# Between the two attentions of a decoder: batch 0's chain alone in front, batch 1's under its scatters and under the first expert items

## The chip, the cores and the metric

One Trainium2 chip, of which one core runs the program. The metric is the device time of one execution in microseconds (us); lower is better. Spans, waits and clocks are from the hardware profiler's record of one execution.

## The reference, cut to what matters

A decoder of two layers on x of 2 x 1024 x 256 (batch, sequence, width), all in float32. What lies between the two self-attentions of the program is the rest of layer 0, and this is the part that is changed:

```python
x = x + _L0_attn_ref(_layernorm(x, axis=-1), ...)             # its last product: s @ w_o
x = x + _L0_xattn_ref(ctx_1024, _layernorm(x, axis=-1), ...)  # a window of 4 out of 77 context rows
x = x + _L0_ffn_ref(_layernorm(x, axis=-1), ...)              # 8 experts, top 2, capacity 320

# cross attention: where a token looks, then scores against 77 context rows
hid = jnp.tanh(jnp.einsum('btc,pc->btp', c_t, W_p))
p_t = Sq * jax.nn.sigmoid(jnp.einsum('btp,op->bto', hid, V_p))
...
gauss = jnp.exp(-jnp.square(s_pos - p_t) / (2.0 * STAN_DEV ** 2))
a_t = jax.nn.softmax(scores, axis=-1) * gauss
s_t = jnp.einsum('btw,btwq->btq', a_t, qw)
# mixture of experts: routing, then a batch's rows of each expert (at most 320), then two matrices up and one down
_, selected_experts = jax.lax.top_k(expert_weights, K)
count_fused = jnp.cumsum(mask_fused, axis=1)
trunc_mask = expert_mask * (count <= capacity).astype(jnp.int32)
h1 = jnp.einsum('ebcm,emh->ebch', dispatch, w1)
h3 = jnp.einsum('ebcm,emh->ebch', dispatch, w3)
expert_out = jnp.einsum('ebch,ehm->ebcm', jax.nn.silu(h1) * h3, w2)
```

The routing of a batch (its running count) needs all 1024 tokens of that batch and none of the other.

## The kernel before

The program runs in stages with a barrier between them: layer 0's attention, then the stage that is called `middle`, then layer 1's attention, then a tail. `middle` handles 16 tiles of 128 tokens, tiles 0 to 7 of batch 0 and 8 to 15 of batch 1, in groups of four tiles (groups 0 and 1 are batch 0's, 2 and 3 batch 1's). Its steps stand in one list, and each engine walks the same list and does its share of each step, so the list sets the order on every engine:

- `turn` and `out`: the attention's heads transposed, times w_o, added to x (TensorE L1534, L1545; VectorE L1808).
- `stat`, `shift`, `norm`: layer norm. VectorE takes mean and variance (L1817 to L1828), ScalarE the root (L1666) and writes the normed rows `xn_nat` (L1674), TensorE transposes them (L1553), ScalarE copies the first half out of PSUM (L1679) and VectorE the second (L1833). Units 0 to 3 are the groups' first norm, units 4 to 7 (`norm 4` and so on) the second, ahead of the experts.
- `hid`, `pos`, `mask`, `score`, `sum`, `flip`, `value`: cross attention (TensorE L1561, L1569, L1576, L1583, L1590). `mask` is thirteen small VectorE instructions in a row (L1841 to L1854), `score` three (L1859 to L1861), `sum` four (L1867 to L1871).
- `logit`, `best`, `cum`, `slot`: routing of a batch (TensorE L1601, L1607 to L1610; VectorE L1788 to L1922). `slot` ends with `idx_s`, the row in DRAM to which each token goes.
- Then GpSimd scatters the batch's normed rows to DRAM (`disp`, L1734) with 16 indirect DMAs.
- An item is one expert with the rows of one batch (320 rows) or of both (640). `rows` loads them from `disp` by SP's queue (L1469) and transposes them (L1619, `xeT`), `ffn` is 7 steps of the two upward products (L1632, four matmuls a batch; a float32 matmul shows as two instructions) with ScalarE's Silu (L1725) and VectorE's product (L1928, `hT`), `y` the downward product (L1642) and its copy (L1944, L1947), which GpSimd stores (L1749).

Weights of two experts are held. SP loads the next expert's upward matrices when TensorE has ended the last `ffn` step of an expert's last item, and the downward one after that item's `y` (L1452, L1455). After the last items GpSimd gathers the results (L1756) and VectorE adds them to x (L1782).

ScalarE holds one table of functions at a time. Tanh and Exp share one, the root and Silu need others, and a copy needs none; a change shows as ACT_TABLE_LOAD.

The list of before has three parts. `lead` is batch 0's chain with `turn 2`, `out 2` and `turn 3` of batch 1 between its steps. `rest` is batch 1's chain from `out 3` to its last `value`; it runs while batch 0 is scattered, and stands ahead of the first `rows` step. `under` is batch 1's second norm and its routing, and is dealt out between the steps of the first item, one TensorE step after each. The items are 12:

```python
    items = [(0, (0,)), (1, (0,)), (0, (1,)), (1, (1,))] + [(e, (0, 1)) for e in range(2, E - 2)] + [
        (E - 2, (0,)), (E - 1, (0,)), (E - 2, (1,)), (E - 1, (1,))]
```

## Time and profile before

| what | us |
|---|---|
| median of 3 runs (lowest, highest) | 1929.97 (1928.99, 1933.12) |
| the profiled execution | 1936.54 |
| its span | 1934.8 |
| granted TensorE clock, mean over the span | 0.906 of full |
| TensorE busy in the span | 1622.1 (84%) |
| VectorE, ScalarE, GpSimd busy | 1049.7, 875.7, 554.9 |

The profiled execution is 1.7 us longer than its span, which runs from its first to its last instruction. The stage `middle` takes from 411.7 us of the span to its barrier at about 1013.7. In the rows below a time at the start of a line is in us from the start of the span. PE is TensorE's matmuls and PEld its weight loads, DVE VectorE, ACT ScalarE, POOL GpSimd, SPq SP's queue. PEclk 1.00 is a granted clock of 2.4 GHz and 0.50 one of 1.2 GHz.

### The profile page before, as it was taken

To read this page: it belongs to the slowest core of one execution; us is meant where nothing else is said; L and a number is where in the kernel's file an instruction comes from. 1 tells how busy PE (TensorE), PEld (TensorE's weight loads), DVE (VectorE), ACT (ScalarE), POOL (GpSimd) and SP (SyncE) were. 2 spreads that over 40 slices of the span, in tenths; PEclk is the share of its full clock that TensorE was granted. 3 is DMA by queue.
4 is the path that set the end of the run, shared out by engine and by line. 5 is a ranking of instruction groups with operands and counts; after the bars stand their busy time and mean duration, and the time that the engine had idled before them with its cause. 6 is when DMAs were issued, how large, how long until landed. Compare 5 with 4: busy or idle time off the path is not lost. (4 is left out here: it accounts for less than half of the span.)

```text
span 1934.8 us, 34483 instructions
## 1 busy us (share of the span) xinstructions
PE 1622.1 (84%) x12814; PEld 1092.5 (56%) x12814; DVE 1049.7 (54%) x2134; ACT 875.7 (45%) x1467; POOL 554.9 (29%) x791
## 2 busy tenths in 40 slices
PE   4668899876576999999927819999999999997888
PEld 2323333335454777777713406777777777776644
DVE  4557777624441111111236328888888888884556
ACT  2115666653231111111106108888888887883431
POOL 2201111110303000000333115556555565553011
PEclk9759999987677999999967659999999999998899
DMA  2541121030101232221213286687786886854100
GB/s 82 124 156 22 22 43 22 2 120 1 51 7 64 84 116 85 84 78 54 64 52 129 82 109 194 181 201 200 204 208 193 205 210 193 201 172 157 72 12 33
DMA packets 207560, 207.44 MB, mean 107 GB/s; under 512 B 20612, under 2 KB 186131, under 8 KB 207267
## 3 DMA queue, kind: packets, MB, share of 16 engines
q1 hardware_dynamic: 202531, 191.61, 37.1%
q0 software_dynamic: 4864, 13.64, 2.1%
q8 instruction: 103, 1.69, 0.4%
q14 instruction: 62, 0.51, 0.1%
HBM read 123.18 MB, written 81.81 MB: 106 GB/s over the span
## 5 line engine op out<-in xcount | busy, mean ns | idle before, releaser
L1174 DVE CUSTOM_DVE_ANT_0 prob<-ps,dev 128x1024 f32<-128x1024 f32 x256 | 311.5, 1218 | 30.3 <-DMA dev<-skew_u 27.4
L1072 ACT ACTIVATE prob<-prob,nmax 128x1024 f32<-128x1024 f32 x256 | 293.5, 1146 | 38.4 <-DVE nmax L1174 38.2
L1004 PE MATMUL ps<-cst,prob 128*128 128x128 f32 x2048 | 279.1, 277 | 1.1 <-ACT probT L1079 0.9
L1004 PEld LDWEIGHTS ps<-cst,prob 128*128 128x128 f32 x2048 | 227.3, 141 | 44.0 <-issue 21.6
L1632 PE MATMUL ps<-xeT,w 128*128 128x320 f32 x896 | 246.8, 436 | 5.0 <-ACT xeT L1713 5.0
L723 ACT ACTIVATE pT<-ps 128x512 f32<-128x512 f32 (+3 forms) x384 | 166.1, 495 | 153.3 <-PE ps L683 150.9
L1188 DVE COPY probT<-ps 128x512 f32<-128x512 f32 x256 | 176.3, 689 | 102.9 <-PE ps L1004 102.9
L760 DVE TENSOR_REDUCE nmax<-ps 128x1 f32<-128x128 f32 (+7 forms) x256 | 185.2, 754 | 82.1 <-PE ps L664 80.9
L1632 PEld LDWEIGHTS ps<-xeT,w 128*128 128x128 f32 x896 | 170.1, 191 | 76.9 <-ACT xeT L1713 5.2
L1079 ACT ACTIVATE probT<-ps 128x512 f32<-128x512 f32 x256 | 151.3, 591 | 102.1 <-PE ps L1004 102.1
L1725 ACT ACTIVATE sg<-ps 128x320 f32<-128x320 f32 (+1 forms) x84 | 44.2, 526 | 330.4 <-PE ps L1632 328.7
L987 PE MATMUL ps<-ks,qs 96*128 96x512 bf16 (+4 forms) x768 | 155.7, 312 | 33.5 <-DVE nmax L1174 22.3
L1928 DVE TENSOR_TENSOR hT<-ps,sg 128x320 f32<-128x320 f32 (+1 forms) x84 | 50.6, 603 | 197.6 <-ACT sg L1725 190.9
L1642 PE MATMUL ps<-w,hT 128*128 128x256 f32 (+1 forms) x616 | 140.7, 388 | 5.9 <-DVE hT L1928 5.8
L662 PE MATMUL ps<-ks,qs 96*128 96x512 bf16 (+3 forms) x384 | 111.5, 356 | 38.1 <-DVE nmax L760 25.4
L1045 PE MATMUL ps<-probT,vg 128*18 128x128 f32 (+1 forms) x4096 | 135.9, 273 | 0.0
L1642 PEld LDWEIGHTS ps<-w,hT 128*128 128x128 f32 (+1 forms) x616 | 112.1, 185 | 31.6 <-DVE hT L1928 7.8
L747 POOL TENSOR_SCALAR_AFFINE_SELECT pT<-pT 128x512 f32<-128x512 f32 x64 | 40.8, 637 | 282.9 <-ACT pT L723 282.9
L683 PE MATMUL ps<-qs,ks 99*128 99x512 bf16 (+3 forms) x384 | 110.2, 337 | 13.6 <-ACT pT L723 7.3
L1045 PEld LDWEIGHTS ps<-probT,vg 128*18 128x18 f32 (+1 forms) x4096 | 106.4, 98 | 17.3 <-issue 16.9
L1749 POOL DMA_DIRECT2D ybuf<-ye x32 | 20.5, 644 | 319.6 <-DVE ye L1944 180.8
L1128 POOL TENSOR_TENSOR wm<-wr,cst 128x256 f32<-128x256 f32 x128 | 94.0, 734 | 43.9 <-DMA wr<-skew_p 41.0
(310 smaller groups left out, 2247.9 us busy)
## 6 DMA issues: line engine op xcount, KB each, us to landing
dev<-skew_u SPq DMA_DIRECT2D x128, 256.0 KB, 3.5
skew_p<-prob SPq DMA_DIRECT2D x128, 256.0 KB, 3.3
w<-in_L_ffn_w SPq DMA_DIRECT2D x24, 896.0 KB, 6.3
skew_u<-cst SPq DMA_DIRECT2D x64, 256.0 KB, 4.1
wr<-skew_p SPq DMA_DIRECT2D x128, 128.0 KB, 3.0
qs<-qd SPq DMA_DIRECT2D x96, 128.0 KB, 3.9
ks<-kd SPq DMA_DIRECT2D x48, 256.0 KB, 6.0
qd<-parts SPq DMA_DIRECT2D x48, 128.0 KB, 1.8
```

The costliest lines, as they stand in the source:

```text
L662: last = nc.tensor.matmul(ps[:, bank, 0:hi - lo], query, ks[0:KS, j, lo:hi], start=True, stop=hi < w)
L723: nc.scalar.activation(pT[:, c % 2, r, 0:w], ps[:, ring_bank(job), 0:w], ACT.Exp).then_inc(s_exp, 1)
L760: nc.vector.tensor_reduce(nmax[:, n % 2, r * KB + a:r * KB + a + 1], slot[:, 0:w], AX.X, ALU.max, negate=True).then_inc(s_max, 1)
L987: last = nc.tensor.matmul(ps[:, 2 * (t % 2) + lo // 512, lo % 512:lo % 512 + hi - lo], qs[:, n % 2, r, a * P:(a + 1) * P], ks[:, n % 2, r, ...
L1004: last = nc.tensor.transpose(ps[:, ring_bank(job), kb * P:(kb + 1) * P], prob_tile(t, (4 * h + kb) * P, (4 * h + kb + 1) * P), k.c("ident"))
L1045: last = nc.tensor.matmul(ps[r * VW:r * VW + wide, 7, q % 4 * P:q % 4 * P + P], vg[:, n % 2, r, kb, int(kb == a), 0:wide], probT[:, (HQ * ...
L1072: nc.scalar.activation(prob_tile(t, 0, S), prob_tile(t, 0, S), ACT.Exp, bias=nmax[:, t % 4:t % 4 + 1], scale=-1.0).then_inc(s_exp, 1)
L1079: nc.scalar.activation(probT[:, t % SLOTS, 0:512], ps[:, ring_bank(job), :], ACT.Copy).then_inc(s_evA, 1)
L1174: nc.vector.tensor_tensor_reduce(out=prob_tile(t, 0, S), in0=scores, in1=dev_tile(t), scale=-1.0, scalar=3.0e38, op0=ALU.add, op1=ALU.min, ...
L1188: nc.vector.tensor_copy(probT[:, t % SLOTS, 512:S], ps[:, ring_bank(job), :]).then_inc(s_evD, 1)
L1632: last = nc.tensor.matmul(ps[:, banks(job)[0] + z * wide + h, 0:CAP], w[:, e % 2, c, f * P:(f + 1) * P], xeT[:, c, h * CAP:(h + 1) * CAP], ...
L1642: last = nc.tensor.matmul(ps[0:w, banks(job)[0] + t // 2, t % 2 * D:(t % 2 + 1) * D], hT[:, f, o:o + w], w2[:, e % 2, f, :], start=(f == 0 ...
```

## The change

`middle` becomes `experts`. Batch 0 and batch 1 get a chain each (class `RowChain`), with buffers and semaphores of their own, and the same steps in the same order (`chain_order`). Batch 0's chain stands in front with nothing of batch 1 in it. Five lots of spare transposes (`warm`: 10, 16, 20, 6 and 20 of the identity, into a bank that nobody reads) stand ahead of five of its steps on TensorE. Then comes batch 1's chain up to `hid 3`, then the first `rows`. All that follows of batch 1's chain is dealt out between the steps of the items, up to two TensorE steps after each. The normed rows are written by GpSimd in place of ScalarE, for both batches, and ScalarE copies both halves of a norm's transposes out of PSUM in place of one. The items are 13: experts 0, 1, 2 for batch 0, then 2, 1, 0 for batch 1, then 3, 4, 5 for both, then 6 and 7 for each. Since the weights of two experts are held, those of expert 0 are loaded a second time, for the sixth item. `sg` and `yg` lie in buffers of batch 0's chain.

```diff
-def middle_order(items):
+def chain_order(b):
...
+    g, h = 2 * b, 2 * b + 1
+    return (two("turn", g) + [("prep", b)] + two("out", g) + two("turn", h) + [("stat", g)] + two("out", h) + [("shift", g), ("stat", h)] +
...
+        kind = step[0]
+        if kind == "shift":
+            u = step[1]
+            at = self.slots(u).start
+            pool.wait_ge(self.s_shift, self.normed.index(u) + 1)
...
+                nc.gpsimd.tensor_scalar(self.xn[:, t, :], k.x[:, KB * self.b + t, :], self.rstd[:, at + j:at + j + 1],
+                                        self.shift[:, at + j:at + j + 1], ALU.mult, ALU.add).then_inc(self.s_xs, 1)
...
+def warmed(steps, where):
+
+    return [s for step in steps for s in ([("warm", where[step], step)] if step in where else []) + [step]]
+
+
+def experts_order(items, lead, chain, ahead):
+
+
+    begun = chain.index(("hid", 3)) + 1
+    under = list(chain[begun:])
+    order = list(lead) + list(chain[:begun]) + [("rows", 0)]
+
+    def deal():
+        singles = 0
+        while under and singles < 2:
+            order.append(under.pop(0))
+            singles += order[-1][0] in RowChain.SINGLE
+
...
+    AHEAD = 3
+    items = ([(e, (0,)) for e in range(AHEAD)] + [(e, (1,)) for e in reversed(range(AHEAD))] +
+             [(e, (0, 1)) for e in range(AHEAD, E - 2)] + [(E - 2, (0,)), (E - 1, (0,)), (E - 2, (1,)), (E - 1, (1,))])
...
+        order = experts_order(items, warmed(chains[0].order, {("norm", 0, 0): 10, ("flip", 0): 16, ("norm", 4, 0): 20, ("norm", 5, 0): 6, ("cum", 0): 20}), chains[1].order, AHEAD)
...
+                for n in range(len(items)):
+                    if n in (0, AHEAD):
+                        sp.wait_ge(chains[n // AHEAD].s_sc, 16 * 2 * KB)
...
+                    if n and last_use[use[n - 1]] == n - 1 and use[n - 1] + 2 < len(loads):
+                        i = use[n - 1] + 2
+                        sp.wait_ge(s_job, done(("ffn", n - 1, FC0 - 1)))
+                        load_up(i)
+                        sp.wait_ge(s_job, done(("y", n - 1)))
+                        load_down(i)
...
+                    if kind == "warm":
+                        for _ in range(step[1]):
+                            nc.tensor.transpose(ps[:, 7, 0:P], k.c("ident"), k.c("ident"))
```

The first place is TensorE in batch 0's chain, from its two `score` steps to its first `logit`. `turned` and `wo` are the `out` step's operands, `x_sc` the scores, `xn_nat` and `xn_c` the normed rows. The row of `cst` alone is a lot of spare transposes. Before:

```order
L1576 MATMUL ps<-gT,xT 128x77 x8
L1561 MATMUL ps<-xT,wpT 100x512 x2
L1569 MATMUL ps<-vp,hidT 128x1 x4
L1534 MATMUL ps<-cst,xT 128x128 x8
L1576 MATMUL ps<-gT,xT 128x77 x8
L1583 MATMUL ps<-cst,x_sc 77x128 x4
L1545 MATMUL ps<-wo,turned 128x256 x8
L1583 MATMUL ps<-cst,x_sc 77x128 x4
L1590 MATMUL ps<-ctxn,aT 128x256 x8
```

and after:

```order
L1473 MATMUL ps<-gT,xT_c 128x77 x8
L1468 MATMUL ps<-vp,hidT_c 128x1 x4
L1473 MATMUL ps<-gT,xT_c 128x77 x8
L1876 MATMUL ps<-cst 128x128 x16
L1477 MATMUL ps<-cst,x_sc_c 77x128 x8
L1481 MATMUL ps<-ctxn,aT_c 128x256 x8
L1876 MATMUL ps<-cst 128x128 x20
L1460 MATMUL ps<-cst,xn_c 128x128 x8
L1486 MATMUL ps<-gateT_c,xT_c 128x8 x8
```

Batch 1's `turn` (L1534) and its `out` of eight matmuls (L1545) are gone from between the steps, the two `flip` steps stand together, and two lots of spare transposes have come in.

The second place is TensorE at the first item. L1632 before and L1902 after are the upward products, `x4` being one of the seven steps of an item with one batch; what stands between them is batch 1's chain. Before, where it is the second norm and `logit`:

```order
L1632 MATMUL ps<-xeT,w 128x320 x4
L1553 MATMUL ps<-cst,xn_nat 128x128 x4
L1632 MATMUL ps<-xeT,w 128x320 x4
L1553 MATMUL ps<-cst,xn_nat 128x128 x4
L1632 MATMUL ps<-xeT,w 128x320 x4
L1601 MATMUL ps<-gateT,xT 128x8 x8
L1632 MATMUL ps<-xeT,w 128x320 x4
```

and after:

```order
L1902 MATMUL ps<-xeT,w 128x320 x4
L1473 MATMUL ps<-gT,xT_c 128x77 x8
L1468 MATMUL ps<-vp,hidT_c 128x1 x4
L1902 MATMUL ps<-xeT,w 128x320 x4
L1473 MATMUL ps<-gT,xT_c 128x77 x8
L1477 MATMUL ps<-cst,x_sc_c 77x128 x4
L1902 MATMUL ps<-xeT,w 128x320 x4
L1477 MATMUL ps<-cst,x_sc_c 77x128 x4
L1481 MATMUL ps<-ctxn,aT_c 128x256 x2
L1902 MATMUL ps<-xeT,w 128x320 x4
L1481 MATMUL ps<-ctxn,aT_c 128x256 x4
```

Scores, `flip` and `value` of batch 1, which stood ahead of the first item, now stand inside it, two steps in each gap.

The third place is GpSimd from batch 0's scatter to batch 1's. `xn_c` are the normed rows, four to a unit, and `ybuf` an item's stored result. Before:

```order
L1734 DMA disp<-xn_nat,idx_s 2688x256 x16
L1741 TENSOR_TENSOR x_gs<-cst,x_pt 128x308
L1744 TENSOR_TENSOR x_gs<-x_gs 128x308
L1741 TENSOR_TENSOR x_gs<-cst,x_pt 128x308
L1744 TENSOR_TENSOR x_gs<-x_gs 128x308
L1734 DMA disp<-xn_nat,idx_s 2688x256 x16
```

and after:

```order
L1562 DMA disp<-xn_c,idx_s_c 2688x256 x16
L1549 TENSOR_SCALAR xn_c<-x,rstd_c,shift_c 128x256 x8
L1554 TENSOR_TENSOR x_gs_c<-cst,x_pt_c 128x308
L1557 TENSOR_TENSOR x_gs_c<-x_gs_c 128x308
L1554 TENSOR_TENSOR x_gs_c<-cst,x_pt_c 128x308
L1557 TENSOR_TENSOR x_gs_c<-x_gs_c 128x308
L1549 TENSOR_SCALAR xn_c<-x,rstd_c,shift_c 128x256 x8
L1949 DMA ybuf<-ye 128x2x256
L1949 DMA ybuf<-ye 64x256
L1562 DMA disp<-xn_c,idx_s_c 2688x256 x16
```

Batch 1's normed rows are now written by GpSimd, and its first eight wait in GpSimd's queue behind the 16 scatters of batch 0.

## Rows read from the trace of the kernel before

**Rows 1.** Windows of the stage: length; PE, PEld, DVE, ACT, POOL busy us (instructions); PEclk, DMA, GB/s.

```profile
411.70:498.30 86.60, 58.36 (x250) 47.17 (x251) 38.53 (x138) 26.41 (x48) 2.85 (x4) 0.70 0.19 67
498.30:550.50 52.20, 28.14 (x112) 20.60 (x110) 27.59 (x94) 15.66 (x32) 18.53 (x20) 0.66 0.16 53
550.50:636.20 85.70, 65.98 (x273) 48.92 (x273) 15.58 (x53) 15.05 (x29) 16.82 (x18) 0.84 0.11 36
636.20:980.40 344.20, 338.25 (x1387) 251.86 (x1386) 63.39 (x103) 47.38 (x92) 33.30 (x44) 1.00 0.24 79
```

**Rows 2.** Timeline, two items of one batch in a row.

```profile
902.73 15.34 PE L1632 MATMUL ps<-xeT,w 128*128 128x320 f32 x56
...
928.60 15.34 PE L1632 MATMUL ps<-xeT,w 128*128 128x320 f32 x56
```

**Rows 3.** Timeline of batch 0's chain: start, duration, engine, line, what.

```profile
439.20 0.16 DVE L1841 TENSOR_SCALAR x_pt<-x_pt 128x4 f32<-128x4 f32 x1
...
443.23 0.48 DVE L1859 TENSOR_TENSOR x_sc<-ps,x_tmp 128x308 f32<-128x308 f32 x1
...
455.18 5.21 PE L1545 MATMUL ps<-wo,turned 128*128 128x256 f32 x16
...
463.08 3.62 PE L1590 MATMUL ps<-ctxn,aT 77*128 77x256 f32 x16
...
473.03 2.10 PE L1553 MATMUL ps<-cst,xn_nat 128*128 128x128 f32 x8 [5.46 <-ACT xn_nat L1674]
...
476.12 3.55 PE L1601 MATMUL ps<-gateT,xT 128*128 128x8 f32 x16 [0.99 <-DVE xT L1833]
...
484.29 3.55 PE L1601 MATMUL ps<-gateT,xT 128*128 128x8 f32 x16 [0.83 <-issue]
...
498.09 0.17 DVE L1922 CAST idx_s<-r_sl 128x16 uint32<-128x16 f32 x1
```

**Rows 4.** Timeline from batch 1's first norm to the first item.

```profile
505.74 2.08 ACT L1674 ACTIVATE xn_nat<-x,shift,rstd 128x256 f32<-128x256 f32 x4
...
515.03 1.93 PE L1561 MATMUL ps<-xT,wpT 128*100 128x512 f32 x4
...
544.12 1.46 PE L1619 MATMUL ps<-cst,xe 128*128 128x128 f32 x6
...
550.58 4.08 PE L1632 MATMUL ps<-xeT,w 128*128 128x320 f32 x8 [5.00 <-ACT xeT L1713]
```

**Rows 5.** Timeline of TensorE's two longer waits in the first items.

```profile
577.29 0.43 PE L1607 MATMUL ps<-r_cand,cst 128*128 128x64 f32 x2 [4.38 <-DVE r_cand L1893]
...
623.15 1.52 PE L1619 MATMUL ps<-cst,xe 128*128 128x128 f32 x6 [15.26 <-DMA xe<-disp]
```

**Rows 6.** Groups by form on GpSimd: busy us, mean ns of one, idle before.

```profile
L215 POOL TENSOR_SCALAR x<-x,inv0a,shift0a 128x256 f32<-128x256 f32 x16 | 8.8, 560 | 28.3 <-ACT xs0a L202 28.3
```

**Rows 7.** Window of the chain's second half.

```profile
473.00:499.00 26.00, 18.73 (x74) 16.45 (x75) 8.34 (x38) 7.90 (x13) 0.43 (x1) 0.50 0.00 1
```

**Rows 8.** Groups by line from 440 to 625 us: busy us, mean ns.

```profile
L1734 POOL DMA_INDIRECT disp<-xn_nat,idx_s x32 | 31.1, 973 | 128.1 <-DVE idx_s L1922 119.0 <-issue 9.1
...
L1601 PE MATMUL ps<-gateT,xT 128*128 128x8 f32 x64 | 10.8, 306 | 1.8 <-DVE xT L1833 1.0 <-issue 0.8
...
L1590 PE MATMUL ps<-ctxn,aT 77*128 77x256 f32 x32 | 10.7, 505 | 0.0
...
L1553 PE MATMUL ps<-cst,xn_nat 128*128 128x128 f32 x48 | 9.7, 353 | 13.2 <-ACT xn_nat L1674 7.1 <-issue 6.0
...
L1576 PE MATMUL ps<-gT,xT 128*128 128x77 f32 x57 | 9.3, 329 | 0.0
...
L1725 ACT ACT_TABLE_LOAD x2 | 2.6, 1283 | 0.0
```

**Rows 9.** Timeline and window of an expert's upward weights being loaded.

```profile
651.56 0.90 SPq L1452 DMA_DIRECT2D w<-in_L_ffn_w  x2
...
654.00:658.00 4.00, 4.00 (x20) 3.51 (x20) 0.00 (x0) 0.00 (x0) 0.00 (x0) 1.00 0.96 393
```

More of the change, by code:

```diff
@@ new lines, in chain_order @@
+    g, h = 2 * b, 2 * b + 1
+    return (two("turn", g) + [("prep", b)] + two("out", g) + two("turn", h) + [("stat", g)] + two("out", h) + [("shift", g), ("stat", h)] +
+            two("norm", g) + [("shift", h), ("hid", g)] + two("norm", h) + [("pos", g), ("hid", h), ("mask", g), ("score", g), ("pos", h),
+            ("mask", h), ("score", h), ("sum", g), ("flip", g), ("sum", h), ("flip", h)] + two("value", g) + [("stat", 4 + g)] +
+            two("value", h) + [("shift", 4 + g), ("stat", 4 + h)] + two("norm", 4 + g) + [("shift", 4 + h), ("logit", g)] +
+            two("norm", 4 + h) + [("logit", h), ("best", b), ("cum", b), ("slot", b)])
@@ L1318, in middle_order @@
             order.append(("ffn", n, f))
[L1319 to L1322 removed]
+            deal()
         if n + 1 < len(items):
@@ L1401, in middle @@
+        own = [s for s in jobs if s[0] not in RowChain.SINGLE]
+        singles = [s for s in jobs if s[0] in RowChain.SINGLE]
+        lead = where[("rows", 0)]
+        split = max(n for n in range(len(items)) if ("ffn", n, 0) in jobs[:where[("cum", 1)]]) + 1
+        assert split <= AHEAD
         xe = k.sb("xe", [P, ST, D], ctx=ctx)
         xeT = k.sb("xeT", [P, DC, ROWS], ctx=ctx)
-        sg = k.sb("sg", [P, 2, ROWS], ctx=ctx)
+        sg = chains[0].xT[:, 0:2, 0:ROWS]
         hT = k.sb("hT", [P, FC0, ROWS], ctx=ctx)
@@ L1422, in pieces, with tenants, place, done @@
+        def tenants(i):
+            return sorted({max(had) for q in bank[i] if (had := [j for j in range(i) if q in bank[j]])})
+        def place(step):
+            return [s for s in own if s[0] == step[0]].index(step) + 1
+        def done(step):
+            return own.index(step) + 1
+        def loaded(n):
+            return sum(i % 2 == use[n] % 2 for i in range(use[n] + 1))
         def pieces(n):
@@ L1948, in _ @@
                         last.then_inc(s_y, 1)
+                    elif kind not in ("rows", "warm"):
+                        chain_of(step).vector(dve, link, step, ps[:, a, :])
                 for t in range(KB, NT):
```

927 lines of the change are left out of this document (453 added, 474 removed).

## The prediction

> **What bounds the kernel now.** I read the windows of the changed stage first, since the other stages' code is untouched. From the third item on, TensorE is busy 338.3 of 344.2 us at the full granted clock [rows 1]: that part is bound by its matmuls, and only their number could change it. Two items of one batch start 25.87 us apart [rows 2]; the stretch holds six such items and four of both batches, so one of both takes (344.2 - 6 x 25.87) / 4 = 47.25. Ahead of it the picture is another. From 411.7 to 550.5 us no item runs, TensorE is busy 58.4 of 86.6 and 28.1 of 52.2 us, and the clock is 0.70 and 0.66 [rows 1]. The bound there is latency: a chain from engine to engine, and the time to look at is when each step of it starts.
>
> The timeline of batch 0's chain shows batch 1 in its way once: `out 2` takes TensorE for 5.2 us from 455.18, between the two `flip` steps, and VectorE's `sum 1` waits behind its additions, so that `value 0` starts only at 463.08 [rows 3]. `idx_s` ends at 498.26. Then the scatter runs, but the first item starts at 550.58, 52.3 us after `idx_s`, because batch 1's `rest` stands ahead of it on TensorE and its normed rows kept ScalarE from `xeT` for 5.0 us more [rows 4]. In the first two items TensorE waits 4.4 us for batch 1's `best`, and 15.3 us for rows of batch 1 that are still being scattered [rows 5]. These two items take 636.2 - 550.6 = 85.6 us where 2 x 25.87 = 51.7 would do: 33.9 too many.
>
> **The change, part by part.**
>
> *Batch 0's chain alone.* Up to `mask 0` (439.20 before) little changes: TensorE's `out` is the same work, and the first layer norm waits for the same additions. The gain there is that the normed rows of group 1 no longer take ScalarE's 2.08 us [rows 4] between `hid 0` and `pos 0`, and that `hid 0` may keep the full clock (1.7, half of a 3.4 us step): some 3.5 together, an estimate, which puts `mask 0` at 435.7. From there I follow the longest dependency: `mask` takes 443.23 - 439.20 = 4.0, `score` three VectorE instructions of 0.48, 1.5 with their gaps [rows 3]. So `score 0` ends at 441.2, Exp 0 and `pos 1` on ScalarE at 441.9, `mask 1` at 445.9, `score 1` at 447.4, `sum 0` and `sum 1` (1.5 each, the same kind) at 450.4, and `value 0` starts at 451.1 in place of 463.08, 12.0 earlier. Behind it stand two `value` additions, `stat 4`, `value 1`, `shift 4` and the normed rows, 9.95 us from `value 0` to `norm 4` before (463.08 to 473.03 [rows 3]); I keep 9 of it, the table load for the root being hidden. Then comes `logit 0` at 461.7 (before 476.12), and after norm 5 `logit 1` at 466.4 (before 484.29: 17.9 earlier). From its start to `idx_s` it was 14.0 us, of which 1.7 is the lower clock in `logit` itself; at the full clock `idx_s` ends at 478.4, 19.9 earlier.
>
> *GpSimd for the normed rows.* The same operation on GpSimd takes 0.560 us [rows 6], against 2.08 / 4 = 0.52 on ScalarE [rows 4]: 0.16 more for four, 0.6 over the chain's four units, inside the rounding above. ScalarE's second copy costs nothing, since its first is done before the second half is transposed.
>
> *The spare transposes.* In the 26 us from 473 to 499 TensorE is busy 18.7 us with transposes, `logit`, `cum` and then `out`, and the clock stays at 0.50 [rows 7]. At 1.2 GHz throughout, the chain above is longer by about half of each TensorE step on it: 1.7 for `hid 0`, 1.7 for each `logit`, 1 for `value`, 2 for norms and flips, and some 2 for the lots of 6 and 20 that no longer fit into TensorE's waits: 10 us. Nothing in the trace shows idle time filled with transposes, so the cost lies between 0 and 10. Before, the chain had 0.70; I take 3, as the waits filled are those next to `value` and `hid`, where the clock did rise. `idx_s` ends at 481.5, **16.8 us earlier**.
> Here the Trainium skill speaks against the change ("TensorE: Matmul & The Clock Gate", section on PE-mode transpose): it says that the full clock does not engage for transposes, so the lots would hold nothing. The row of 473 to 499 agrees, but mixes in other steps. By the rule the sum would be 7 less; I keep it as a rival.
>
> *From `idx_s` to the first item.* 16 scatters of (31.1 + 9.1) / 32 = 1.26 [rows 8] and 0.5 to start: 20.6. Batch 1's normed rows stand behind them on GpSimd, and TensorE's `norm 2` and the first item's `rows` behind those. Before, from the normed rows of unit 2 (505.74) to the end of `hid 3` (516.96) it was 11.2 [rows 4]; with GpSimd 11.4. `rows` takes 1.5, its copy 0.8, with ScalarE free. The item's rows need only the scatter and SP's load, which end before. Together 34.3 in place of 52.3: **18.0 us less**, and the first item starts at 515.8.
>
> *Batch 1's chain inside the items.* Before, its `rest` lay ahead of them; now it costs TensorE's time between their steps. Its work from `score 2` on, from the groups by line [rows 8]: `logit` half of 10.8, `value` half of 10.7, transposes 16 of 48 of 9.7, scores 32 of 57 of 9.3, `cum` 3 and small ones 1: 23 at that mixed clock, 20 at a mostly full one. To it come waits, as the item's Silu and product stand in the same queues as the chain. VectorE has, after the first step's product, `mask 2` and `score 2` (5.5), then Exp, the table load of 1.28 [rows 8] and Silu and product of step 2 (3.0), then `mask 3`, `score 3` and `sum 2` (7.0): 15.5 until `flip 2` may start, against 6 us of TensorE's work in that time (scores, `pos`, one item step): a wait of 9.7. The next are `sum 3` behind the third product, 2.5; `norm 6` behind `value`, `stat`, `shift` and GpSimd, 4 (5.46 before, with nothing to cover it [rows 3]); `best` ahead of `cum`, 3.7 (4.4 before [rows 5]). Sum 20, and 3 for the clock after such waits. The excess over steady items is 20 + 20 + 3 = 43, where it was 33.9: **9.1 us more**. The wait of 15.3 for the scatter is in the 33.9 and doesn't return: batch 1's `idx_s` comes about 75 us after the first item's start, its rows 25 us later, and item 4 wants them at about 112.
>
> *The items themselves.* Ten of one batch and three of both are 10 x 25.87 + 3 x 47.25 = 400.5, where 8 x 25.87 + 4 x 47.25 = 396.0: **4.5 us more** (six tiles of the downward product in place of five, and one more round). The second load of expert 0 is issued when the fifth item's `ffn` ends and wanted after its `y`, 25.87 - 15.34 = 10.5 us later. Such a load was issued at 651.56 and was moving at 393 GB/s by 658 [rows 9]; 1.8 MB at that rate is 4.7 us. It is hidden, with 4 us to spare; without that cover it would cost its 6.5.
>
> **Sum:** -16.8 - 18.0 + 9.1 + 4.5 = -21.2 on a span of 1934.8, so 1913.6. The profiled execution, 1936.54, was 6.6 above the median of the runs, so for the median 1929.97 - 21.2 = 1908.8: **1909 us**.
>
> **Rivals.**
> 1. *The spare transposes hold no clock.* The chain costs 10 in place of 3: 1916. For it speaks the 0.50 from 473 to 499, against it that `value` next to two of the lots is matmul work. 0.15.
> 2. *The chain runs at the full clock and the waits inside the items are short* (3 for the clock twice, and two or three of the waits): 1901. Nothing in the trace excludes it. 0.13.
> 3. *The reload of expert 0 is exposed*, since SP is held by a wait ahead of it or the load is slowed by stores: +6, 1915. The rows at 651.56 speak against it. 0.05.
> 4. *Slower.* The chain inside the items locks step with them: each of some nine item steps that have chain steps behind them waits for VectorE and ScalarE, with two table loads of 1.28 and a `mask`-like run each time. It decides when the excess passes 43 + 21 = 64 us, that is, when TensorE waits 41 us instead of 20. With all of it doubled, 1930 to 1935. Against it: before, six such steps were passed with a single wait of 4.4. 0.04.
> 5. *No change.* The same mechanism as in 4, near its turning point of 64: 0.02.
>
> **How the numbers follow.** The forecast as such has 0.61 and a range of its own from 1903 to 1915, from the unknown 0 to 10 of the clock and half of the 20 us of waits. The range for 8 in 10 reaches to rivals 1 to 3: 1898 to 1921. A difference under 0.2% (3.9 us) is about what a measurement of this kernel can't tell from no change. Slower by more has rival 4's 0.04, within it 0.02, faster 0.94.
>
> **What would show each step.** `idx_s` of batch 0 at 481 (478 to 488); the first item's upward product at 516; TensorE's longest wait in it, of some 10 us, ahead of `flip 2`, ended by VectorE; `mask` and `score` of batch 1 behind the products on VectorE; no wait of TensorE for `xe` at item 4; none for weights at item 6; the steady stretch at 25.87 an item, ending about 960. The prediction is wrong if the waits inside the items come to over 30 us, if `rows` of item 1 waits for `xe`, or if the granted clock stays at 0.50 through the chain.

## The result and the profile after

The changed kernel takes 1920.5 us, the median of 7 runs from 1913.4 to 1924.7, where the kernel before took 1932.8 (7 runs, 1929.0 to 1935.0). The ratio is 0.9937, with a 95% interval from 0.9924 to 0.995: 12.3 us faster. The forecast was 1909, with 1898 to 1921 for 8 in 10, so the time lies at the upper edge of that range. Of all runs reported here one, an execution of e9 of 2210.6 us at a mean granted clock of 0.717, is left out of its kernel's ratio.

I compare places by their distance from SyncE's first load of the stage, which starts at 411.66 us before and at 410.81 after. Batch 0's chain first, in the timeline of the changed kernel (start, duration, engine, line, operation; in brackets the idle time ahead and who ended it):

```profile
430.20 3.62 PE L1465 MATMUL ps<-xT_c,wpT 128*100 128x512 f32 x4 [0.69 <-ACT xT_c L1516]
...
451.65 7.03 PE L1481 MATMUL ps<-ctxn,aT_c 77*128 77x256 f32 x16
...
463.77 1.95 PE L1486 MATMUL ps<-gateT_c,xT_c 128*128 128x8 f32 x16 [0.69 <-ACT xT_c L1516]
...
468.04 1.95 PE L1486 MATMUL ps<-gateT_c,xT_c 128*128 128x8 f32 x16 [0.74 <-ACT xT_c L1516]
469.85 3.31 PE L1876 MATMUL ps<-cst 128*128 128x128 f32 x20
```

and in VectorE's:

```profile
480.24 0.17 DVE L1689 CAST idx_s_c<-r_sl_c 128x16 uint32<-128x16 f32 x1
```

`value 0` starts 40.8 us from the stage's start, in [rows 3] 51.4, so 10.6 earlier. It takes 7.03 us where it took 3.62, and each `logit` 1.95 where it took 3.55: the half clock has changed its place. The first line is `hid 0`, whose 3.62 us are the half clock too. `idx_s` ends at 69.6 us, before at 86.6: 17.0 earlier. From there to the first item, and the three items with batch 1's chain in them, TensorE's timeline shows this:

```profile
502.12 2.19 PE L1460 MATMUL ps<-cst,xn_c 128*128 128x128 f32 x8 [13.23 <-POOL xn_c L1549]
...
513.90 2.42 PE L1902 MATMUL ps<-xeT,w 128*128 128x320 f32 x8 [0.85 <-ACT xeT L1927]
...
532.66 1.14 PE L1477 MATMUL ps<-cst,x_sc_c 128*77 128x128 f32 x4 [9.76 <-DVE x_sc_c L1643]
533.59 3.50 PE L1902 MATMUL ps<-xeT,w 128*128 128x320 f32 x8
539.62 1.14 PE L1477 MATMUL ps<-cst,x_sc_c 128*77 128x128 f32 x4 [2.53 <-DVE x_sc_c L1643]
...
542.26 4.28 PE L1902 MATMUL ps<-xeT,w 128*128 128x320 f32 x8
...
555.21 1.12 PE L1460 MATMUL ps<-cst,xn_c 128*128 128x128 f32 x4 [3.92 <-POOL xn_c L1549]
556.12 4.18 PE L1902 MATMUL ps<-xeT,w 128*128 128x320 f32 x8
...
583.92 0.69 PE L1489 MATMUL ps<-r_cand_c,cst 128*128 128x64 f32 x2 [3.74 <-DVE r_cand_c L1663]
...
587.36 16.91 PE L1902 MATMUL ps<-xeT,w 128*128 128x320 f32 x56
```

The first upward product stands at 513.90, 33.5 us after `idx_s`, where it was 52.3 [rows 4]. The four waits of 9.76, 2.53, 3.92 and 3.74 us are those that the prediction listed, ended by the engines that it named; the wait of 15.26 for scattered rows [rows 5] is gone. But right behind these waits the same eight matmuls take 3.50, 4.28 and 4.18 us, where at the full clock they take 2.3, and a whole item's upward product 16.91 instead of 15.34. The windows of chain, mixed items and steady items say it in another way (length; busy us of PE, PEld, DVE, ACT, POOL; granted clock, DMA share, GB/s):

```profile
410.80:480.50 69.70, 58.16 (x295) 47.95 (x296) 34.92 (x135) 18.37 (x33) 11.55 (x20) 0.74 0.24 84
...
513.90:640.70 126.80, 105.26 (x441) 78.66 (x441) 39.05 (x128) 31.59 (x52) 25.40 (x32) 0.87 0.16 54
640.70:963.40 322.70, 317.04 (x1299) 234.51 (x1298) 60.52 (x103) 44.90 (x91) 31.91 (x42) 1.00 0.25 83
```

The three mixed items take 126.8 us for 3 x 25.87 = 77.6 of their own, an excess of 49.2, with a clock of 0.87. The steady stretch is at 1.00, as before [rows 1], and what is in it takes what [rows 2] say.

By parts, after less before: chain -17.0, gap -18.8, excess +15.3, items +4.5, in sum -16.0; the stage as a whole goes from 602.0 to 586.1 us, which is -15.9. The span of the profiled run falls by 13.9 only: the stage starts 0.9 us earlier, and the stages behind, whose code is the same, took 924.0 us instead of 921.1. Over the fourteen kernels profiled here that remainder lies between 917.7 and 927.9 with identical code and a mean of 922.9, so that 3 us are within what one execution differs from another.

### The profile page after: what moved, and what is told of

Same layout as the page of the kernel before. It is cut to its first block and busy times, and to the rows that moved or that the text cites. A ratio compares the mean times of both kernels' runs of the same rounds, so it can differ in the third digit from the quotient of the medians.

```text
span 1920.9 us, 34708 instructions
## 1 busy us (share of the span) xinstructions
PE 1632.7 (85%) x12904; PEld 1099.1 (57%) x12904; DVE 1047.0 (55%) x2139; ACT 874.4 (46%) x1458; POOL 572.3 (30%) x823
## 5 line engine op out<-in xcount | busy, mean ns | idle before, releaser
L1902 PE MATMUL ps<-xeT,w 128*128 128x320 f32 x896 | 253.8, 444 | 0.9 <-ACT xeT L1927 0.9
L1004 PEld LDWEIGHTS ps<-cst,prob 128*128 128x128 f32 x2048 | 227.5, 141 | 42.6 <-issue 20.5
L1902 PEld LDWEIGHTS ps<-xeT,w 128*128 128x128 f32 x896 | 174.2, 196 | 75.6 <-issue 8.4
L1939 ACT ACTIVATE xT_c<-ps 128x320 f32<-128x320 f32 (+1 forms) x91 | 45.4, 499 | 329.8 <-PE ps L1902 329.8
L1995 DVE TENSOR_TENSOR hT<-ps,xT_c 128x320 f32<-128x320 f32 (+1 forms) x91 | 51.7, 568 | 224.5 <-ACT xT_c L1939 224.5
L747 POOL TENSOR_SCALAR_AFFINE_SELECT pT<-pT 128x512 f32<-128x512 f32 x64 | 40.8, 637 | 282.5 <-ACT pT L723 282.5
L1949 POOL DMA_DIRECT2D ybuf<-ye x32 | 20.5, 644 | 323.5 <-DVE ye L2012 187.4
```

The costliest lines, as they stand in the source:

```text
L1004: last = nc.tensor.transpose(ps[:, ring_bank(job), kb * P:(kb + 1) * P], prob_tile(t, (4 * h + kb) * P, (4 * h + kb + 1) * P), k.c("ident"))
L1902: last = nc.tensor.matmul(ps[:, a + z * wide + h, 0:CAP], w[:, j, c, f * P:(f + 1) * P], xeT[:, c, h * CAP:(h + 1) * CAP], start=(c == 0), ...
```

## The experiments

Twelve kernels, all small edits of the changed one. Start, stage and remainder are read from SyncE's loads in each profile; `idx_s` is batch 0's, the first item is its first upward product, both counted from the stage's first load. The ratio is to the kernel before on the same chip.

| kernel | idx_s | first item | stage | remainder | median us | ratio (95%) |
|---|---|---|---|---|---|---|
| before | 86.6 | 138.9 | 602.0 | 921.1 | 1932.8 | |
| changed | 69.6 | 103.1 | 586.1 | 924.0 | 1920.5 | 0.9937 (0.9924-0.995) |
| e1 no spare transposes | 73.6 | 106.9 | 589.6 | 923.2 | 1927.0 | 0.9968 (0.9957-0.9979) |
| e2 spare matmuls | 72.5 | 106.5 | 586.4 | 920.6 | 1923.8 | 0.9955 (0.9942-0.9968) |
| e3 cut behind score 3 | 69.8 | 114.4 | 588.4 | 917.7 | 1919.3 | 0.9930 (0.9917-0.9943) |
| e4 two split first | 69.9 | 103.4 | 599.2 | 924.0 | 1935.1 | 1.0005 (0.9993-1.0016) |
| e5 ScalarE's rows | 69.8 | 97.2 | 578.9 | 924.6 | 1915.6 | 0.9918 (0.9904-0.9933) |
| e6 both chains first | 70.0 | 148.7 | 584.6 | 922.5 | 1919.1 | 0.9920 (0.9907-0.9933) |
| e7 e5 with e3 and banks | 69.2 | 102.5 | 571.7 | 921.2 | 1908.7 | 0.9876 (0.9861-0.989) |
| e8 spare in the items | 69.2 | 103.1 | 575.8 | 923.8 | 1908.2 | 0.9866 (0.9851-0.988) |
| e9 e5, both first, two split | 68.3 | 134.1 | 565.6 | 923.2 | 1903.3 | 0.9844 (0.9831-0.9856) |
| e10 e9 with more spare | 69.9 | 130.2 | 559.6 | 923.0 | 1894.4 | 0.9800 (0.9787-0.9813) |
| e11 e7 with more spare | 70.0 | 100.1 | 562.5 | 924.3 | 1895.8 | 0.9812 (0.9799-0.9824) |
| e12 56 at the first flip | 69.0 | 103.0 | 582.8 | 927.9 | 1920.3 | 0.9929 (0.9911-0.9948) |

Every stage in this table is one execution. Worked out from the ratios and 1932.8 us, the distances from the changed kernel are +6.0 us for e1, +3.5 for e2, -1.4 for e3, +13.1 for e4, -3.7 for e5, -3.3 for e6, -11.8 for e7, -13.7 for e8, -18.0 for e9, -26.5 for e10, -24.2 for e11 and -1.5 for e12. They differ from the stage's by up to 3.7 us, so a stage that is shorter or longer by less than some 4 us shows nothing alone. A place in a timeline that many kernels have in common is firmer.

### e1 and e2: what the spare transposes do

```diff
-        ... warmed(chains[0].order, {("norm", 0, 0): 10, ("flip", 0): 16, ("norm", 4, 0): 20, ...}) ...
+        ... warmed(chains[0].order, {}) ...
```

> All 72 spare transposes of batch 0's chain are left out, nothing else. My reading of the changed kernel (they neither raise nor hold the clock, and lie in waits): the chain ends within 1.5 us of where it did (idx_s 69.6 us after the stage's first load), the time stays within 0.1% of the changed kernel, 1918 to 1923. Rival (they hold TensorE's clock): the mean granted clock of the chain falls from 0.74 to about 0.65 and idx_s comes 3 to 7 us later, time 1923 to 1928. Third: they cost time, being on the path before the cum step, and the chain gets 1 to 3 us shorter.

For e2 the spare instruction is another:

```diff
-                            nc.tensor.transpose(ps[:, 7, 0:P], k.c("ident"), k.c("ident"))
+                            nc.tensor.matmul(ps[:, 7, 0:P], k.c("ident"), k.c("ident"), start=True, stop=True)
```

> The 72 spare transposes become 72 spare matmuls of the same 128x128 tile. The Trainium skill's page 'TensorE: Matmul & The Clock Gate', by its section on transposes, has it that transposes don't raise the clock and matmuls do: by that rule the chain's half-clock stretches (448 to 460 and 471 to 481.5 of the trace, the value steps in 7.0 us where they took 3.6 before, and the cum step) go to full clock, idx_s comes 4 to 6 us earlier, time about 1915. Rival (the kind of the spare instruction doesn't matter, the chip lets the clock fall after a wait whatever follows): within 1.5 us of the changed kernel, 1919 to 1922.

My expectation for e1 fell. Without the spare transposes `idx_s` comes 4.0 us later, the stage is 3.5 longer, and the intervals of the ratios don't touch. In the eleven kernels with spare transposes in batch 0's chain `idx_s` ends 68.3 to 70.0 us from the stage's start, in e1 at 73.6. The timeline of e1 for the chain's second half:

```profile
465.02 3.58 PE L1486 MATMUL ps<-gateT_c,xT_c 128*128 128x8 f32 x16 [0.69 <-ACT xT_c L1516]
...
471.09 3.58 PE L1486 MATMUL ps<-gateT_c,xT_c 128*128 128x8 f32 x16 [0.69 <-ACT xT_c L1516]
...
478.89 3.10 PE L1492 MATMUL ps<-r_cand_c,cst 128*128 128x56 f32 x14
```

Both `logit` steps take 3.58 us where the changed kernel's take 1.95. The windows of e1 and of the changed kernel at the same places show why:

```profile
458.00:460.00 2.00, 1.48 (x4) 0.50 0.00 0
...
462.00:464.00 2.00, 1.86 (x8) 0.50 0.00 0
...
482.00:484.00 2.00, 2.00 (x10) 0.50 0.00 0
```

```profile
458.00:460.00 2.00, 2.00 (x10) 0.50 0.00 0
460.00:462.00 2.00, 2.00 (x16) 0.78 0.00 0
462.00:464.00 2.00, 1.31 (x11) 1.00 0.00 0
```

The columns are length, busy us (instructions), granted clock, DMA share, GB/s. In both kernels the clock falls to 0.50 in the wait ahead of the first flip and stays there through the `value` steps, though TensorE is busy without a gap. In the changed kernel the 20 spare transposes of 458.48 follow without a gap, and at 461 the clock is up; in e1 a wait of 2.65 us follows, then waits of 0.69, 0.69 and 3.74, and the clock is still at 0.50 at 484. So transposes, put in behind matmuls where a wait would be, do bring the full clock back in this chain. The prediction had weighed against this the Trainium skill's sentence on transposes ("TensorE: Matmul & The Clock Gate", section on PE-mode transpose), by which the full clock doesn't engage for them; as a statement on what spare transposes can do in such a chain, this pair contradicts it.

e2 doesn't reach the 1915 of the rule either. From its timeline:

```profile
457.20 6.62 PE L1876 MATMUL ps<-cst 128*128 128x128 f32 x40
...
469.07 1.92 PE L1460 MATMUL ps<-cst,xn_c 128*128 128x128 f32 x8
```

Its 72 spare matmuls show as 144 matmul records and take twice the time: the 40 of 457.20 last 6.62 us and hold up norm 4, which starts 2.1 us later than in the changed kernel, counted from the start of the stage. `value` still takes 7.03 us. Behind it both `logit` steps have the full clock, norm 5 hasn't (1.92 us in place of 1.04), and `cum` has it again (1.68 in place of 3.10). But `idx_s` comes 2.9 later, and its ratio is a little above the changed kernel's, with intervals that meet. The profiled execution was the fastest of its five (1919.3 against a median of 1923.8), so its stage of 586.4 flatters it.

### e3: batch 1's cut moved back

```diff
-    begun = chain.index(("hid", 3)) + 1
+    begun = chain.index(("score", 3)) + 1
```

> Batch 1's chain is cut behind score 3 instead of hid 3: its pos, mask and score steps of both groups stand ahead of the first rows. Theory (the waits in the items are the DVE mask chain started too late): first ffn about 4 us later (three small steps at half clock ahead of it), the 9.8 and 2.5 us waits for the flips shrink to about 6 in sum, 4.8 us of work leaves the items; sum about -7, time 1912 to 1915. Rival (the DVE chain is the bound in any order, the wait only changes its place): -3 to 0, 1917 to 1921. The clock can add 3 us either way.

The stage is 2.3 us longer, the time the same: 1919.3, which the rival had, but not by its mechanism. Most of the wait left the flips and went ahead of the rows:

```profile
521.32 1.49 PE L1890 MATMUL ps<-cst,xe 128*128 128x128 f32 x6 [5.92 <-DVE x_sc_c L1634]
523.66 4.39 PE L1902 MATMUL ps<-xeT,w 128*128 128x320 f32 x8 [0.85 <-ACT xeT L1927]
530.52 0.66 PE L1477 MATMUL ps<-cst,x_sc_c 128*77 128x128 f32 x4 [2.46 <-DVE x_sc_c L1643]
```

The first item's `rows` wait 5.92 us until VectorE is done with batch 1's score step (`x_sc_c`), which has just had their banks; the first item starts 11.3 us later, not 4. Neither theory named this: the steps that stand ahead of the cut hold up an item through the banks they leave.

### e4: two experts split first

```diff
-    AHEAD = 3
+    AHEAD = 2
```

> Two experts are split first instead of three: 12 items, no expert is loaded twice at that place, batch 1's chain all within two items. Theory: the third item's rows stand ahead of the second item's down step and wait some 15 us for batch 1's scatter (TensorE stands), the items' work itself is 4.5 us less (2 times 25.87 against 47.25), the clock after that wait costs 1 to 3: +11 to +14, time 1931 to 1934. Rival (the scatter isn't what is late, since it only has to be there by 615): 4.5 us faster, 1916.

The stage is 13.1 us longer, inside the expected 11 to 14, and the gain over the kernel before is gone. TensorE's timeline:

```profile
618.75 1.52 PE L1890 MATMUL ps<-cst,xe 128*128 128x128 f32 x6 [15.28 <-DMA xe<-disp]
```

It is the wait of [rows 5] again, 15.28 us for rows of batch 1. So the third split expert costs 4.5 us of item work and saves a wait of 15.3 and the clock behind it (11.30 us for a downward product that takes 9.45 at the full clock). The prediction counted it so.

### e5: the normed rows back on ScalarE for batch 1

Only the units 2 and 3 (batch 1's first norm, ahead of its cross attention) change their engine:

```diff
+        elif kind == "shift" and step[1] in (2, 3):
...
+                nc.scalar.activation(self.xn[:, t, :], self.k.x[:, KB * self.b + t, :], ACT.Identity, bias=self.shift[:, at + j:at + j + 1],
+                                     scale=self.rstd[:, at + j:at + j + 1]).then_inc(self.s_xs, 1)
...
-        if kind == "shift":
+        if kind == "shift" and step[1] not in (2, 3):
```

> Only the first of the three edits of the run with ScalarE's rows and the later cut: groups 2 and 3 get their normed rows from ScalarE, the cut stays behind hid 3. Theory (the two edits pay only together: the earlier rows let TensorE run ahead to the cut, where it then stands until the expert's rows come in at 512, and VectorE's mask chain still starts behind the first ffn step): TensorE's 13.2 us wait moves from norm 2 to the first rows, the waits at the flips stay at 9.8 and 2.5 us, stage 0 to 2 us shorter, time 1918.5 to 1921. Rival (the 14 us of that run came from ScalarE's rows alone): 1906 to 1910.

7.2 us off the stage, where I expected 0 to 2 and the rival 14: 5.9 at the first item, 1.3 behind it. Both fell. The 5.9 are firm, since the first item starts at 103.0 to 103.4 us in the changed kernel, e4, e8 and e12, which have the same order and queues up to there; the ratios show 3.7 us, with intervals that meet. TensorE's timeline:

```profile
491.09 0.71 PE L1460 MATMUL ps<-cst,xn_c 128*128 128x128 f32 x4 [2.19 <-ACT xn_c L1516]
...
505.58 1.52 PE L1898 MATMUL ps<-cst,xe 128*128 128x128 f32 x6 [3.98 <-DMA xe<-disp]
507.96 4.42 PE L1910 MATMUL ps<-xeT,w 128*128 128x320 f32 x8 [0.85 <-ACT xeT L1935]
```

The wait of 13.23 us at norm 2 is 2.19. I had taken it that the expert's rows come in at 512, because the changed kernel starts its `rows` there; that was the time at which TensorE asked for them. With the queue of scatters off its path TensorE asks at 501.6 and has them at 505.58. So 6 of the 33.5 us between `idx_s` and the first item were no need of the item: they were the normed rows behind the scatters on GpSimd and TensorE's five steps behind these, from norm 2 to `hid 3`. The prediction saw that queue and priced it rightly, and took it as given.

### e6: both chains in front

```diff
-    begun = chain.index(("hid", 3)) + 1
+    begun = len(chain)
```

The count of items that overlap the chain, which sets the banks, is set to one.

> All of batch 1's chain stands ahead of the first rows, nothing of it lies inside the items. In the changed kernel the first three items carry 49.2 us beside their own 77.6, and batch 1's chain, once its first normed rows are there at 502, should need what batch 0's needed from there to its cum step, about 50 us. Theory (inside the items the chain's waits stand as bare as in front, so the mixing hides nearly nothing): first ffn at about 555 instead of 514, the three items in 78 to 80 us, fourth item's ffn near 634 instead of 640.7: time 1912 to 1917. Rival (the mixing does hide work): fourth item's ffn at 650 or later, 1929 or more.

The stage is 1.5 us shorter than the changed one, and the time, 1919.1, lies between the two expectations and can't be told from the changed kernel's. The first item starts 45.6 us later, and the three items take 79.6 us (559.21 to 638.82), which is 2.0 more than their own, the first upward product being 17.37 us at the lower clock. So the rest of batch 1's chain costs 45.6 us standing bare in front, and cost 49.2 mixed with the items: in the changed kernel the mixing hides next to nothing (49.2 against 45.6 + 2.0). It couldn't be seen from the prediction's sum, which priced work and waits of the mixed order and never asked what the other order would cost.

### e7: ScalarE's rows, later cut, banks of its own

e5's edit, e3's edit, and batch 1's steps in banks 4 to 7 only:

```diff
-                return [i % 7 if i < lead else 4 + singles.index(jobs[i]) % 4]
+                return [i % 7 if singles.index(jobs[i]) < len(chains[0].jobs) else 4 + singles.index(jobs[i]) % 4]
```

> Three edits: the normed rows of groups 2 and 3 (batch 1, before the experts' gate) are made on ScalarE and not on GpSimd behind batch 0's 16 scatters; the cut stands behind score 3; batch 1's steps use banks 4 to 7 alone. Theory (TensorE's 13.2 us wait at 502 is GpSimd's queue of scatters, and the waits inside the items come from starting the mask chain after it): norm 2 at about 490, the mask chain of VectorE runs while the expert's rows come in, first rows still at 512, the 9.8 and 2.5 us waits at the flips gone, 4.8 us of work out of the items: -12 to -17, time 1904 to 1909. Rival (the flip also needs GpSimd's mask, which still queues behind the scatters, or the waits only go one step on): -3 to -6, 1915 to 1918.

14.4 us off the stage, as the first theory had it (11.8 by the ratios; the profiled execution was 4.5 below the median). 7.2 are e5's, so the cut and the banks together bring 7.2, where the cut alone cost 2.3. Which of the two brings it isn't separated; no wait stands ahead of the `rows` any more, which in e3 was 5.92. TensorE's timeline:

```profile
504.82 0.86 PE L1898 MATMUL ps<-cst,xe 128*128 128x128 f32 x6
512.10 4.64 PE L1910 MATMUL ps<-xeT,w 128*128 128x320 f32 x8 [6.41 <-ACT xeT L1935]
519.20 1.14 PE L1477 MATMUL ps<-cst,x_sc_c 128*77 128x128 f32 x4 [2.46 <-DVE x_sc_c L1651]
```

`flip 2` waits 2.46 us, `flip 3` 0.49. A new wait stands ahead of the first item, 6.41 us for `xeT`. In ScalarE's timeline its copies stand behind the Exp of batch 1's `score 3`, which waits for VectorE:

```profile
510.93 0.46 ACT L1537 ACTIVATE x_sc_c<-x_sc_c 128x308 f32<-128x308 f32 x1 [3.44 <-DVE x_sc_c L1642]
511.30 0.74 ACT L1935 ACTIVATE xeT<-ps 128x512 f32<-128x512 f32 x2
```

### e8: spare transposes in the waits of the items

```diff
-        order = experts_order(items, warmed(...), chains[1].order, AHEAD)
+        order = experts_order(items, warmed(...), warmed(chains[1].order, {("flip", 2): 60, ("flip", 3): 16, ("norm", 6, 0): 24, ("cum", 1): 24}), AHEAD)
...
-                return [i % 7 if i < lead else 4 + singles.index(jobs[i]) % 4]
+                return [i % 7 if i < lead else 4 + singles.index(jobs[i]) % 3]
```

> The changed kernel with 124 more spare transposes in batch 1's chain: 60 ahead of flip 2, 16 ahead of flip 3, 24 ahead of norm 6, 24 ahead of its cum step (in the waits of 9.8, 2.5, 3.9 and 3.7 us); the chain's small steps use banks 4 to 6, bank 7 takes the spare ones. Theory (the term that I mis-sized is the clock after these waits: four steps of 3.5 to 4.3 us instead of 2.3 and a start of 16.9 instead of 15.3, some 9 us): the granted clock of the first three items goes from 0.87 to 0.95 or more and they take 4 to 8 us less, time 1913 to 1917. Rival (spare transposes leave the clock as it is): 0 to +3, as far as they don't fit the waits, 1920 to 1924.

This is the run for the mis-sized term. The stage is 10.2 us shorter, more than the 4 to 8 expected, and all of it lies between the first item and the fourth. The window of these three items, and TensorE's timeline:

```profile
512.30:628.70 116.40, 108.45 (x564) 84.81 (x564) 39.08 (x128) 31.47 (x52) 25.46 (x32) 0.99 0.18 59
```

```profile
521.12 6.71 PE L1876 MATMUL ps<-cst 128*128 128x128 f32 x60
531.05 0.89 PE L1477 MATMUL ps<-cst,x_sc_c 128*77 128x128 f32 x4 [3.22 <-DVE x_sc_c L1643]
531.74 3.82 PE L1902 MATMUL ps<-xeT,w 128*128 128x320 f32 x8
...
539.45 2.32 PE L1902 MATMUL ps<-xeT,w 128*128 128x320 f32 x8
...
577.00 15.32 PE L1902 MATMUL ps<-xeT,w 128*128 128x320 f32 x56
```

`flip 2` starts 18.8 us after the first item in both kernels: the spare work doesn't delay it. The step right behind `flip 2` gains nothing (3.82 us, in the changed kernel 3.50): 3.22 us of the wait were left bare, and the clock fell there. But over the three items the granted clock goes from 0.87 to 0.99, the item's later steps are 2.32 to 2.40 us, `cum` 1.68, the upward product 15.32, and the three items take 116.4 us: an excess of 38.8 instead of 49.2. The prediction's 20 us of work and 20 of waits, in sum, fit this to 1.2. The ratios, 0.9866 against 0.9937 without overlap, bear it out, and the time, 1908.2, is below the 1913 to 1917 expected. The edit also takes one of four banks from batch 1's small steps; no run has that alone.

### e9: both chains first, two experts split, ScalarE's rows

e7 with `begun = len(chain)` and `AHEAD = 2`; the count of overlapping items is set to one as in e6.

> ScalarE's normed rows for groups 2 and 3 and the banks as in e7, all of batch 1's chain ahead of the first rows as in e6, and two experts split first instead of three. Theory (the mixing hides nearly nothing, GpSimd's queue costs batch 1's chain 10 us): idx_s of batch 1 at about 545, first ffn at about 543, no excess in the items, 4.5 us less of item work, no wait for batch 1's scatter (in by 567, wanted at 584): stage 20 to 24 us shorter, time 1896 to 1901. Rival (the chain of batch 1 has the wait anyway, through GpSimd's masks and the second normed rows): 8 to 12 us shorter, 1909 to 1913.

20.5 us off the stage, inside the first theory's 20 to 24; the time, 1903.3, is above its 1896 to 1901. `AHEAD = 2`, which cost 13.1 us in e4, brings no wait here: TensorE goes from item to item without one for rows, since batch 1's `idx_s` ends at 544.6 and the third item's rows are wanted at 587.0. What the split costs depends on the order it stands in.

### e10, e11: filling every wait

More spare transposes in both chains, in the order of e9 (e10) and in that of e7 (e11); the steps keep off bank 7, which the spare ones write. For that e10 has batch 1's steps in seven banks where e9 has them in four, and e11 in three. e11's lots for batch 1 are 18, 24, 24, 6 and 34. e10:

```diff
-        ... {("norm", 0, 0): 10, ("flip", 0): 16, ("norm", 4, 0): 20, ("norm", 5, 0): 6, ("cum", 0): 20}), chains[1].order, AHEAD)
+        ... {("norm", 0, 0): 18, ("flip", 0): 56, ("norm", 4, 0): 22, ("norm", 5, 0): 6, ("cum", 0): 30}), warmed(chains[1].order, {("norm", 2, 0): 18, ("flip", 2): 60, ("norm", 6, 0): 22, ("norm", 7, 0): 6, ("cum", 1): 30}), AHEAD)
```

> Batch 1's chain all in front, two experts split, ScalarE's rows, as in the run before (1903.3), and more spare transposes, so that each wait of TensorE in both chains is filled: 56 ahead of the first flip instead of 16, 18, 22, 6 and 30 at the other places, and 18, 60, 22, 6 and 30 in batch 1's chain, which had none. Theory (a wait that is left bare costs the clock of what follows): the value steps 7.0 to about 4 us in both chains, batch 1's logit steps 3.6 to 1.95, its cum step 3.1 to 1.7, the first item's up steps 17.6 to about 15.4; -10 to -14 in the stage, time 1889 to 1894. Rival (spare work delays the steps behind it as much as the clock gives): 1900 to 1904.

> The same filling of the waits in the version that mixes batch 1's chain, cut behind score 3, with three items (1908.7): 18, 24, 24, 6 and 34 spare transposes in batch 1's chain, 56 at the first flip. Theory: half-clock steps in the items (4.6, 3.9, 4.1, 3.1, 11.4 us where 2.3, 2.3, 2.3, 1.7 and 9.5 would do) go for the most part, and 4 us in batch 0's chain: -8 to -11, time 1898 to 1901. Against the other order at full clock it tells what mixing is worth: if it hid work, it would end nearer to 1889.

e10 takes 1894.4 us, 0.98 of the kernel before, and is the fastest here; e11 takes 1895.8, and their intervals overlap. e11's stage is 9.2 us shorter than e7's, as expected. e10's gain over e9 is 6.1 us in the stage, half of what I expected (the time just misses its 1889 to 1894, e11's is below its 1898 to 1901), and its timeline says where it is and where it isn't:

```profile
449.20 3.62 PE L1481 MATMUL ps<-ctxn,aT_c 77*128 77x256 f32 x16
...
466.24 3.58 PE L1486 MATMUL ps<-gateT_c,xT_c 128*128 128x8 f32 x16 [0.69 <-ACT xT_c L1524]
...
512.98 7.03 PE L1481 MATMUL ps<-ctxn,aT_c 77*128 77x256 f32 x16
...
529.36 1.95 PE L1486 MATMUL ps<-gateT_c,xT_c 128*128 128x8 f32 x16 [0.74 <-ACT xT_c L1524]
...
540.41 15.34 PE L1910 MATMUL ps<-xeT,w 128*128 128x320 f32 x56 [0.85 <-ACT xeT L1935]
```

The first item has its full clock from the start (15.34, in e9 17.58), and batch 1's `logit` and `cum` take 1.95 and 1.68 (3.58 and 3.10 in e9). But in batch 0's chain `value` now takes 3.62 and `logit 1` 3.58: the half clock came later, and `idx_s` isn't earlier. Counted from the stage's start, e10 is 4 us ahead of the changed kernel at norm 4 and still 1.2 ahead at `logit 1`. Then the 30 spare transposes, most of them at the half clock, take 5.59 us and hold up the `cum` step, which starts 2.0 us later: spare work costs time where it outlasts the wait. And batch 1's `value` took 7.03 with its wait filled. With the waits filled the mixed order, with 4.5 us more of item work, is 3.0 us of stage behind the other. By that mixing would save 1.5 us, which is less than two executions differ: no gain of mixing is shown.

### e12: the wait at the first flip

```diff
-{..., ("flip", 0): 16, ...}
+{..., ("flip", 0): 56, ...}
```

> The changed kernel with one number other: 56 spare transposes ahead of batch 0's first flip instead of 16, so that the wait of 5.5 us that is left bare there is about 0.7. Theory: the clock doesn't fall at 448, the value steps take about 4 us instead of 7.0, the spare transposes behind them 2.3 instead of 3.5: idx_s 3.5 to 4.5 us earlier, time 1915.5 to 1917. Rival (the clock falls there for another reason than the wait): idx_s where it was, 1919.5 to 1921.

The theory fell, in its own kernel:

```profile
441.82 6.28 PE L1876 MATMUL ps<-cst 128*128 128x128 f32 x56
449.23 0.66 PE L1477 MATMUL ps<-cst,x_sc_c 128*77 128x128 f32 x4 [1.13 <-DVE x_sc_c L1643]
...
451.73 7.03 PE L1481 MATMUL ps<-ctxn,aT_c 77*128 77x256 f32 x16
```

```profile
446.00:448.00 2.00, 2.00 (x20) 1.00 0.00 0
448.00:450.00 2.00, 0.76 (x5) 1.00 0.00 0
450.00:452.00 2.00, 1.15 (x5) 0.73 0.00 0
```

The wait is down from 5.5 to 1.13 us, and the clock falls all the same, at 450.9, 3.7 us later than in the changed kernel. Just before, TensorE had four transposes between waits of 1.13 and 0.96 us. `value` takes 7.03, `idx_s` is 0.6 us earlier, and the time is the changed kernel's. In e10 and e11 the same filling was followed by a `value` at full clock. The stage is 3.3 us shorter all the same, nearly all of it in the mixed items, whose code is untouched (513.56 to 637.07, 123.5 us for 126.8; a step of 4.28 us in the changed kernel takes 2.77 here): the granted clock of this stretch is 0.89 for 0.87, so this much can come and go with the clock in these items from one execution to another.

## Why the prediction was right, and where it was off

*Batch 0's chain: 16.8 said, 17.0 measured.* The size is right, its parts partly by luck. `mask 0` came 25.0 us from the stage's start, said 24.0 (435.7 - 411.66): `hid 0`, which was to keep the full clock, took 3.62 us, and in e1, without the lot of ten ahead of norm 0, it took the same. The 3 us for the clock were to be spread over the chain. `value 0` is 1.4 us later than the sum had it without them, norm 4 2.6 and `idx_s` 2.9; in the trace the half clock lies on `hid 0`, on `value` (7.03 instead of 3.62) and on `cum` (3.10 instead of 1.68), while both `logit` steps had the full clock. Rival 1, that the spare transposes hold nothing, is refuted by e1, but its price was too high: the prediction had 7 us between the two cases, and e1 shows 4.0 of chain and 3.5 of stage.

*From `idx_s` to the first item: 18.0 said, 18.8 measured*, by the queue that the prediction described. From `idx_s` to the first upward product 34.3 us were said and 33.5 came. e5 shows that 6 us more were to be had there.

*Batch 1's chain in the items: +9.1 said, +15.3 measured.* This is the step that was off. The four waits were said as 9.7, 2.5, 4 and 3.7 and are 9.76, 2.53, 3.92 and 3.74. (The first is a slip that came out well: the prediction's own 15.5 less 6 is 9.5, and the Exp and the table load that it names are not in its 15.5.) The term was "3 for the clock after such waits". By e8 against the changed kernel it is 10.4 (126.8 against 116.4 us, with `flip 2` at the same distance), and by e8 against e12, whose items are those of the changed kernel, 7.1. Both are differences of single executions, and in e8 the half clock is not quite gone either (the step of 3.82). I had sized it as if only the chain's own small steps ran at half speed; but an item's steps stand behind these waits, and each matmul of them takes twice as long until the clock is back: 1.2 + 2.0 + 1.9 us on the three steps shown, 1.6 on the upward product, and the rest in the steps between.

*The items: +4.5 said.* The stretch from the fourth item on fits 25.87 an item; the upward matrices of expert 0 are asked for at 681.89 and TensorE takes them up at 692.38 without a wait, so rival 3 did not come. e4 shows the 15.3 us that the third split expert avoids.

*The sum.* The time is 11.7 us above the 1908.8 said, outside the forecast's own 1903 to 1915, and within 1898 to 1921 by 0.5 us only; that margin had been set by rivals 1 to 3, none of which came. 2.8 of the 11.7 are the base, since the kernel before has a median of 1932.8 over seven runs where the three at hand gave 1930.0; 5.3 are the stage, and 3.6 lie between the stage and the medians. For the stage -21.2 was said and -15.9 measured: the excess was 6.2 worse than said, chain and gap together 1.0 better. The stages behind added 2.9 in the profiled pair, which is chance by the fourteen remainders above. The distance between the medians, 12.3, is 3.6 less than the stage's 15.9. The changed kernel's runs spread over 11.3 us, those of before over 6.0; e12 shows 3.3 us of items that come and go with the clock (0.89 for 0.87), and the remainders differ by as much and more at a mean clock of 0.92 in all fourteen, so theirs has another cause that isn't shown. What of either is in the medians isn't shown.

*Rivals 2, 4 and 5* needed short waits or an excess of some 64 us; the waits came as said, and the excess was 49.2. None of the three signs named for a wrong prediction came: the waits in the items are 20 us, `rows` of item 1 wait for nothing, and the clock doesn't stay at 0.50 through the chain.

*Open.* What makes the clock fall in batch 0's chain. e12, e10 and e11 have the same steps there and the same 56 spare transposes ahead of the flip, and `value` takes 7.03 us in the first and 3.62 in the other two. Up to there they differ in 10 and 18 ahead of norm 0, some 16 us before the lot at the flip; with 18 `hid 0` has the full clock too (1.96 us against 3.63). But in e10's batch 1, with 18 and 60 at the same places and `hid 2` at 1.96, `value` takes 7.03 again, so the lot of 18 isn't the whole answer, and no run changes it alone. Filling waits with transposes held the clock through most of the items (e8) and brought it back at 458 (changed against e1), but neither keeps it for sure through a chain with gaps.
